# Second attention: the first sequence's output tiles projected inside the loop, and one PSUM bank for the output

## What is computed

```
q, k, v = x @ Wq, x @ Wk, x @ Wv        # 32 query heads, 8 key heads, head width 16
q, k = rope(q), rope(k)
scores = q @ k.T / 4, masked above the diagonal
ctx = softmax(scores) @ v               # (tokens, 512)
x = layernorm(x + ctx @ Wo)
# fourth block: x @ weight.T plus a low-rank part of two chosen experts out of eight
h = x @ gw1.T + gb1 ; gates from h ; x = layernorm(x + main + lora)
```

## Time and profile before

| what | value |
|---|---|
| median of 3 runs | 1127.17 us |
| profiled execution | 1127.07 us |
| its span, first to last instruction | 1125.3 us |
| TensorE busy | 1094.8 us (97%) |
| VectorE busy | 731.9 us (65%) |
| ScalarE busy | 635.4 us (56%) |
| GpSimd busy | 458.1 us (41%) |
| TensorE clock granted | 0.998 of full |
| loop of the third block | ends at 1045.34 us of the span |

### The profile page before, as it was taken

One profiled execution on the slowest core, in us unless ns is written; L12 is line 12 of the kernel. 1 busy time (PEld: TensorE's weight loads), 2 busy tenths in 40 slices (PEclk: granted clock), 3 DMA queues, 4 the chain that ended last, 5 costly groups with the idle time before them and its releaser, 6 DMA issues. The chain is left out here.

```text
span 1125.3 us, 19409 instructions
## 1 busy us (share of the span) xinstructions
PE 1094.8 (97%) x6288; PEld 898.7 (80%) x6288; DVE 731.9 (65%) x2384; ACT 635.4 (56%) x1487; POOL 458.1 (41%) x471
## 2 busy tenths in 40 slices
PE   7999999999999999999999999999999999999997
PEld 5888888888888888888888877888888875555786
DVE  6767776667776657776667776222242689997675
ACT  6656665556666556665566554454320237878424
POOL 4654554354544354553445251333310336345300
PEclk9999999999999999999999999999999999999999
DMA  6011110011111011110110000222200246661001
GB/s 240 20 38 39 38 39 29 13 38 38 39 38 29 13 47 38 32 35 29 28 30 20 29 1 24 80 75 69 96 5 1 36 55 86 92 110 20 1 1 75
DMA packets 28566, 49.72 MB, mean 44 GB/s; under 512 B 4400, under 2 KB 5552, under 8 KB 28464
## 3 DMA queue, kind: packets, MB, share of 16 engines
q1 hardware_dynamic: 27888, 47.41, 17.7%
q10 hardware_dynamic: 576, 1.05, 0.3%
HBM read 38.35 MB, written 2.10 MB: 36 GB/s over the span
## 5 line engine op out<-in xcount | busy, mean ns | idle before, releaser
L497 POOL TENSOR_TENSOR turned<-turned,sin 128x512 f32<-128x512 f32 x73 | 94.5, 1294 | 309.6 <-ACT turned L357 309.6
L373 ACT ACTIVATE probs<-probs,neg_max 128x256 f32<-128x256 f32 (+1 forms) x256 | 119.8, 473 | 11.3 <-DVE neg_max L590 11.3
L1748 DVE CUSTOM_DVE_ANT_0 a_unused<-bank,a_mask 128x512 bf16<-128x512 f32 (+3 forms) x256 | 109.1, 487 | 5.1 <-PE bank L1964 4.4
L500 POOL TENSOR_TENSOR turned<-turned,by_cos 128x512 f32<-128x512 f32 x73 | 101.2, 1386 | 5.7
L96 PE MATMUL bank<-wo_hi,oT_hi 128*128 128x512 f32 x256 | 100.3, 392 | 1.7 <-DVE oT_lo L653 1.7
L744 PE MATMUL bank<-xT_hi,wq_hi 128*128 128x512 f32 x256 | 101.5, 396 | 0.0
L744 PE MATMUL bank<-xT_lo,wq_hi 128*128 128x512 f32 x256 | 100.2, 391 | 0.0
L744 PE MATMUL bank<-xT_hi,wq_lo 128*128 128x512 f32 x256 | 100.1, 391 | 0.0
L96 PE MATMUL bank<-wo_hi,oT_lo 128*128 128x512 f32 x256 | 99.9, 390 | 0.0
L96 PE MATMUL bank<-wo_lo,oT_hi 128*128 128x512 f32 x256 | 99.7, 389 | 0.0
L432 ACT ACTIVATE pT_hi<-bank 128x512 fp32r<-128x512 f32 x112 | 61.7, 595 | 52.4 <-PE bank L783 52.4
(11 more groups left out here) (248 smaller groups left out, 3170.1 us busy)
## 6 DMA issues: line engine op xcount, KB each, us to landing
staged<-weights SPq DMA_DIRECT2D x70, 256.0 KB, 2.7
f_staged<-weights_f SPq DMA_DIRECT2D x33, 256.0 KB, 2.7
a_q_stack<-a_qT_hi SPq DMA_DIRECT2D x32, 128.0 KB, 3.4
rows<-x_rows SPq DMA_DIRECT2D x2, 1024.0 KB, 7.3
a_q_stack<-a_qT_lo SPq DMA_DIRECT2D x16, 128.0 KB, 3.9
out<-rows SPq DMA_DIRECT2D x8, 256.0 KB, 2.0
a_raw<-weights_qkv SPq DMA_DIRECT2D x4, 384.0 KB, 5.1
probs<-weights SPq DMA_DIRECT2D x4, 256.0 KB, 5.0
```

Of the source, the lines that this page charges most:

```text
L373: act.activation(probs[:, s % 2, h, 0:width], probs[:, s % 2, h, 0:width], ACT.Exp, bias=neg_max[:, s % 2, h:h + 1], scale=SCALE0, accum_o ...
L497: pool.tensor_tensor(at, at, sin[:, :], ALU.mult).then_inc(sin_done, 1)
L500: pool.tensor_tensor(at, at, by_cos_at(a, first), ALU.add).then_inc(roped, 1)
L1748: dve.tensor_tensor_reduce(unused[:, UNUSED_AT[qt]:UNUSED_AT[qt] + seen], ps_s[bank][:, at:at + seen], mask[:, SEQ - seen:SEQ], 1.0, LOWES ...
```

## The change

From slot 39 on, every 6 slots, one output tile of the first sequence is turned (`turn_early`, in the first of the 6 slots), split by ScalarE and VectorE in that slot, projected in four parts of 3 matmuls (`project_early`, in the third to sixth slot), and added to the rows by VectorE (`add_early`, in the sixth). All of this uses bank 7. So `ps_o` has bank 6 alone, `apply(u, 0)` waits for `join(u - 1)`, and `turn_tops` goes behind `apply` and writes into unused columns of bank 5, with a wait for that slot's exponentials; `key_scores` waits in its last piece of slots s % 4 = 2 for the copy of the tops. After the loop only tiles 4 to 7 are projected, the lists of three engines are reordered, and the fourth block's weight gets its high part from GpSimd instead of ScalarE. The diff, without the lines that only follow from `ps_o` being one bank, and with most removed lines of the last part left out (they stand in the kernel above):

```diff
@@ -1238,7 +1238,7 @@
...
-OUT_AHEAD = 58
+EARLY_FROM, EARLY_EVERY, EARLY_PARTS = 39, 6, 4
@@ -1367,9 +1367,10 @@
...
-        ps_s, ps_t, ps_o = psum[0:3], psum[3:6], psum[6:8]
-        ps_top = [psum[5]] + [ps_o[(u + 1) % 2] for u in range(1, UNITS1)]
+        ps_s, ps_t, ps_o = psum[0:3], psum[3:6], psum[6]
+        ps_top = [psum[5][:, 0:P]] + [psum[5][:, 2 * P:3 * P] for u in range(1, UNITS1)]
...
+        ps_early = psum[7]
@@ -1435,8 +1436,14 @@
...
+        def early_step(s):
+
+            tile, step = divmod(s - EARLY_FROM, EARLY_EVERY)
+            return (tile, step) if 0 <= tile < SEQ_TILES else (None, None)
...
+            bank = ps_early if tile < SEQ_TILES else ps_out[tile % 2]
@@ -1578,8 +1585,9 @@
...
-                if OUT_AHEAD <= s < OUT_AHEAD + SEQ_TILES:
-                    high_out(s - OUT_AHEAD)
+                tile, step = early_step(s)
+                if step == 0:
+                    high_out(tile)
@@ -1601,25 +1609,33 @@
...
-            act.wait_ge(main_raised, KC)
-            for k in range(KC):
-                act.activation(main_hi[:, k, :], main_raw[k], ACT.Copy).then_inc(main_hi_done, 1)
-            act.wait_ge(side_in, 32)
-            act.activation(b_hi[:, :], b_raw[:, :], ACT.Copy).then_inc(main_hi_done, 1)
-            for tile in range(TILES):
...
+            for tile in range(SEQ_TILES):
                 norm2.root(act, tile)
-                if tile >= 3:
-                    gate_root(tile - 3)
+            evacuate(UNITS1 - 1)
+            norm2.high(act, 0)
+            norm2.high(act, 1)
+            high_out(4)
+            high_out(5)
+            side_rows(0)
+            norm2.high(act, 2)
+            side_rows(1)
+            norm2.high(act, 3)
+            norm2.root(act, 4)
+            side_rows(2)
+            high_out(6)
+            norm2.root(act, 5)
+            side_rows(3)
+            high_out(7)
+            act.wait_ge(main_lo_done, KC)
+            norm2.high(act, 4)
@@ -1697,9 +1713,11 @@
...
             for k in range(KC):
+                pool.tensor_copy(main_hi[:, k, :], main_raw[k]).then_inc(main_hi_done, 1)
                 pool.wait_ge(main_hi_done, k + 1)
                 pool.tensor_tensor(main_lo[:, k, :], main_raw[k], main_hi[:, k, :].bitcast(F32),
                                    ALU.subtract).then_inc(main_lo_done, 1)
+            pool.tensor_copy(b_hi[:, :], b_raw[:, :]).then_inc(main_hi_done, 1)
@@ -1790,6 +1808,10 @@
...
+            def add_early(tile):
+                dve.wait_ge(y_ready, tile + 1)
+                dve.tensor_tensor(rows[:, tile, :], ps_early[:, :], rows[:, tile, :], ALU.add).then_inc(y_added, 1)
...
                 if s % GROUP1 == 1 and s >= 2 * GROUP1 + 1:
...
-                if OUT_AHEAD <= s < OUT_AHEAD + SEQ_TILES:
-                    low_out(s - OUT_AHEAD)
+                tile, step = early_step(s)
+                if step == 0:
+                    low_out(tile)
+                if step == EARLY_EVERY - 1:
+                    add_early(tile)
@@ -1813,12 +1838,15 @@
...
+            def take_stats(tile):
+                dve.wait_ge(y_added, tile + 1)
+                norm2.take(dve, tile)
+                norm2.moments(dve, tile)
@@ -1868,19 +1896,41 @@
...
-            for tile in range(TILES):
...
+            for tile in range(SEQ_TILES - 1):
+                take_stats(tile)
+            join(UNITS1 - 2)
+            take_stats(SEQ_TILES - 1)
+            for tile in range(SEQ_TILES):
                 norm2.scale(dve, tile)
-                if tile >= 3:
-                    gate_scale(tile - 3)
+            join(UNITS1 - 1)
+            norm2.split_low(dve, 0)
+            norm2.split_low(dve, 1)
+            low_out(4)
+            gate_rows(0)
+            low_out(5)
+            gate_rows(1)
+            norm2.split_low(dve, 2)
+            gate_scale(0)
+            gate_scale(1)
+            add_output(4)
+            norm2.split_low(dve, 3)
+            norm2.scale(dve, 4)
+            gate_rows(2)
+            low_out(6)
+            gate_scale(2)
+            add_output(5)
+            gate_rows(3)
+            norm2.scale(dve, 5)
+            low_out(7)
+            gate_scale(3)
+            add_output(6)
+            norm2.scale(dve, 6)
+            norm2.split_low(dve, 4)
+            add_output(7)
+            norm2.split_low(dve, 5)
+            gate_rows(4)
+            norm2.scale(dve, 7)
+            gate_scale(4)
@@ -1975,6 +2025,8 @@
...
+                if piece == PIECES - 1 and h == 2 and u + 1 < UNITS1:
+                    pe.wait_ge(top_ready, u + 2)
@@ -1987,14 +2039,9 @@
...
-                if u == 1:
-                    pe.wait_ge(v_done, TILES)
-                    pe.wait_ge(sin_done, 4 * TILES)
-                if u == 2:
-                    pe.wait_ge(part_lo, len(TURNS))
-                if u >= 3:
-                    pe.wait_ge(finished, u - 2)
-                pe.transpose(ps_top[u][:, 0:P], tops[:, u % 2, :], ident[:, :]).then_inc(top_turned, 1)
+                else:
+                    pe.wait_ge(exp_done, PIECES * (GROUP1 * u - 2))
+                pe.transpose(ps_top[u], tops[:, u % 2, :], ident[:, :]).then_inc(top_turned, 1)
@@ -2002,11 +2049,9 @@
...
-                if u == 1 and part == 0:
-                    pe.wait_ge(part_lo, len(TURNS))
                 if part == 0:
-                    if u >= 2:
-                        pe.wait_ge(finished, u - 1)
+                    if u >= 1:
+                        pe.wait_ge(finished, u)
@@ -2097,9 +2142,32 @@
...
+            def turn_early(tile):
+                pe.wait_ge(finished, KV1)
+                if tile >= 1:
+                    pe.wait_ge(y_added, tile)
+                for k in range(KC):
+                    mm = pe.transpose(ps_early[:, k * P:(k + 1) * P], o_tok[:, tile, k * P:(k + 1) * P],
+                                      ident[:, :])
+                mm.then_inc(out_turned, 1)
+
+            def project_early(tile, part):
+
+                at = slice(tile * P, (tile + 1) * P)
+                if part == 0:
+                    pe.wait_ge(w_lo_done, 3 * KC)
+                    pe.wait_ge(out_lo, tile + 1)
+                steps = [(a, b, k) for k in range(KC) for a, b in ((outT_hi, wo_hi), (outT_hi, wo_lo), (outT_lo, wo_hi))]
+                each = len(steps) // EARLY_PARTS
+                for n in range(part * each, (part + 1) * each):
+                    a, b, k = steps[n]
+                    mm = pe.matmul(ps_early[:, :], a[:, k, at], b[:, k, :], start=(n == 0), stop=(n == len(steps) - 1))
+                if part == EARLY_PARTS - 1:
+                    mm.then_inc(y_ready, 1)
@@ -2141,8 +2209,6 @@
...
-                if s % GROUP1 == 1 and s + 3 < SLOTS1:
-                    turn_tops((s + 3) // GROUP1)
@@ -2154,29 +2220,40 @@
...
+                if s % GROUP1 == 1 and s + 3 < SLOTS1:
+                    turn_tops((s + 3) // GROUP1)
...
-            pe.wait_ge(w_lo_done, 3 * KC)
-            for tile in range(TILES):
-                project_out(tile)
...
+                tile, step = early_step(s)
+                if step == 0:
+                    turn_early(tile)
+                if step is not None and step >= EARLY_EVERY - EARLY_PARTS:
+                    project_early(tile, step - (EARLY_EVERY - EARLY_PARTS))
+            turn_output(UNITS1 - 2)
+            for part in range(APPLY_PARTS):
+                apply(UNITS1 - 1, part)
+            norm2.turn(pe, 0)
+            norm2.turn(pe, 1)
+            turn_output(UNITS1 - 1)
+            pe.wait_ge(max_done, SEQ_TILES * SLOTS1)
+            turn_out(4)
+            pe.wait_ge(side_lo_done, KC)
+            side(0)
+            turn_out(5)
+            side(1)
+            norm2.turn(pe, 2)
+            project_out(4)
+            norm2.turn(pe, 3)
+            side(2)
+            turn_out(6)
+            project_out(5)
+            side(3)
+            turn_out(7)
+            project_out(6)
+            norm2.turn(pe, 4)
+            project_out(7)
+            norm2.turn(pe, 5)
+            side(4)
```

More of the change, by code:

```diff
@@ L1436, in maxima_before @@
             return ROW_TILES.index(qt) + 1
+        def early_step(s):
+            tile, step = divmod(s - EARLY_FROM, EARLY_EVERY)
+            return (tile, step) if 0 <= tile < SEQ_TILES else (None, None)
         def out_bank(tile):
-            return ps_out[tile % 2][:, :].rearrange("p (k c) -> p k c", k=KC)
+            bank = ps_early if tile < SEQ_TILES else ps_out[tile % 2]
+            return bank[:, :].rearrange("p (k c) -> p k c", k=KC)
         @block.sync
@@ L1602, in scale_last, with side_rows @@
                                scale=last.inv_deviation[:, tile:tile + 1]).then_inc(last.normed, 1)
[L1604 to L1622 removed]
+            def side_rows(tile):
+                low_rows(tile)
+                gate_root(tile)
+            for tile in range(SEQ_TILES):
+                norm2.root(act, tile)
+            evacuate(UNITS1 - 1)
```

(55 more changed lines are left out.)

21 lines of the change are left out of this document (6 added, 15 removed).

## The result

The changed kernel takes 1138.34 us (median of 4 runs, 1137.42 to 1140.88) against 1127.43 (1126.89 to 1127.84): a ratio of 1.0101, 95% interval 1.0082 to 1.0119. The profiled execution took 1137.5 us with a span of 1135.8; before it was 1127.07 with 1125.3. So 10.4 us came in between these two executions, where 10.2 were forecast; the forecast was 1137.

The account below looks back on a forecast made before the run. TensorE was taken as the bound, with VectorE nearly as full in the loop. Loop +14.2, last part -7.3, collision +2.0, entries +1.0 and tops +0.3 gave +10.2 on 1127.07: 1137 us, range 1130 to 1143.

Parts of the forecast that it names:

- The bound: Slots 39 to 63: TensorE's 3.0 us of stand-still is all that moved work can fill; the loop grows by 14.2 us.
- 1.0 for entries: TensorE entering another kind of matmul, for 16 parts of the moved projection: 1.0 us, bounds 0 to 3.2.
- hand-made schedule: Slots 39 to 63, each engine in its order, timed from slot 39's start: 5.9 us of stand-still, end at 63.1.
- The last part: From the loop's end to the gates' transposition: 11.1 us of matmuls leave, 4.0 of stand-still comes, -7.3 us.
- the collision: Behind the loop, GpSimd's casts and subtractions delay VectorE's four norm2.scale before join(15): 2.0 us, bounds 0 to 4.7.
- no collision, 1135 us: Rival: behind the loop GpSimd's casts fall between VectorE's scales, all else as forecast; 1135 us (1131 to 1138), chance 0.20.
- The tops: The moved turn_tops and its copy in the loop: 0.3 us, bounds 0 to 6.
- Slots 9 to 38 I leave as they are: Loop before early projecting: no change, since turn_tops waited for the same join at the place where apply waits now.
- a sign of being wrong: Stated beforehand: the prediction would be wrong if slots 9 to 38 take another time than before the change.
- rival of late tops (+6): Tops' transfer 0.75 us late in eight units of slots 9 to 39, the loop slips: 1143 us, chance 0.13.
- Faster: Rival: loop loses nothing and the last part has no holes either: -3.0 us, 1124 us, chance 0.04.
- gaps filled: Rival: VectorE hides its copies, loop work 57.2 against 48.87; with a last part that waits 1128 us, chance 0.08.

Follow-up runs that it names:

- e1_low_later: The changed kernel with VectorE's low_out of an early tile one slot later, behind the next slot's maxima; 1.28 us less between turn_output of units 7 and 14.

## Why the forecast held, and where it was off

- **The bound.** The loop grew by 15.0, with 14.2 and some of the 1.0 for entries forecast, and the new waits stand in the slots that were named. The hand-made schedule can be held against the trace from slot 39's start: `apply(9, 0)` 6.15 (said 6.3), the first tile's last projecting matmul ends at 15.34 (15.3), the loop's end 63.9 (63.1 before entries). Head-of-line waits in VectorE's list, an instruction that waits and holds up those behind it, are shown by three kernels, with 2.0 us that a mere reordering takes back.
- **The last part.** -5.65 against -7.3 + 2.0. The waits were 0.81 for `evacuate(14)` (said 0.85), 0.81 for `join(14)` (1.4: VectorE's statistics were just done, so the part of it for its order fell away), 0.85 for `join(15)` (1.0, and the collision's 2.0 ahead of it), 0.53 before `side(4)` (0.6). That is 3.0 us of stand-still where 6.0 were said; another 1.6 went into `apply` of unit 15 at half the clock, a term that the sum didn't have. In e1_low_later, without the half clock, the waits come to 4.1 and the last part takes 31.10, -5.9. The work beside the waits takes 1.0 to 1.3 more than the 25.7 that the forecast left it (36.98 - 11.1 - 0.2); the sum had 1.0 for entries, in a term of its own. That the forecast of the last part agrees to 0.3 is in part luck: too much stand-still stood against a half clock and longer work.
- **The collision.** The size was right: 1.9 on four instructions, said 2.0. Its worth on the path was not: GpSimd held back gave 1.34 at the first `side`, and at the gates 0.10, because its last three instructions then met `gate_scale`. The rival "no collision, 1135 us" is therefore not excluded as a mechanism, since seven of GpSimd's ten instructions ran beside VectorE without loss there; but by these figures a list that avoids both places would win some 1.3 us, not 2.0 (an estimate; not run).
- **The tops.** The mis-sized step: 0.3, measured 0.7 in A (0.5 to 1.3 over nine traces of the same code). "Slots 9 to 38 I leave as they are" was wrong, and the prediction had named another time there as a sign of being wrong. So was its reason: I compared the `join` that both kernels wait for, and not the place of `turn_tops` behind `apply` and behind the slot's exponentials, which the diff adds as a wait. Their own bank, ahead of `apply`, takes 2.2 us out of A. The rival of late tops (+6) named a late transfer; only two in slots 8 to 36 came too late for the keys, 0.5 us of wait. The loss was TensorE's own stand at `turn_tops` and at `apply`.
- **The clock.** It was not in the sum. In both profiled executions of the changed kernel its stretch lay where the collision held VectorE anyway, 0.24 us; seven of the ten executions took 1.5 to 3.5 us longer, at a lower mean clock. The forecast of 1137 is therefore that of an execution of the first kind (1137.4 to 1137.6), and the median of 1138.3 holds some of the others.
- **Faster or gaps filled** did not come: by the prediction's own count of the loop's work (57.2) TensorE's stand-still there grew from 3.0 to 6.7 us, and even with every wait that these runs found reordered the kernel stays at 1131.6.

## What to carry to other kernels

When work moves into a loop whose engines are both nearly full, count the room of the loop (3.0 us here) against what moves (11.1), and then look at what stands at the head of each list: a copy that waits for another engine holds the join behind it, and a single buffer passes that on at once. Two uses that share a bank set each other's order: a bank of their own for the tops, and with it a place ahead of `apply`, was worth 2.2 us in slots 8 to 36, and with that the output's second bank was missed only where a `join` stood late in VectorE's list. Moving a helper's work away from one collision is worth nothing if it lands on the next: look up which of the other engine's instructions it will run beside. Covering a wait can be worth more than the wait, since a sparse stretch of TensorE may be followed by 3.4 us at half the granted clock (1.98 us of waiting cost 3.6).

## What the runs showed of the hardware

- TensorE's granted clock fell to 0.50 (1.2 GHz) behind stretches with some work in them (busy 0.43, 0.66 and 0.29 of three microseconds; 0.17 of 2.00 us and then 1.3 us of work in another kernel; 0.94 and 0.80 of two microseconds in a third), and came back to 1.00 after some 3.4 us; `apply` of unit 15 took 3.94 us in it and 2.36 without. The Trainium skill, "TensorE: Matmul & The Clock Gate", "Part 1: The HAM clock gate", has recent activity decide between these two levels. These rows show the two levels; that the same waits came with and without the fall, no run here explains.
- VectorE's small instructions collide with GpSimd too: 128x32 took 1.07 instead of 0.30 us beside a subtraction of 128x512 on GpSimd. In each collision here VectorE's instruction ended shortly behind GpSimd's, 0.28 us at 128x512 and about 0.04 at 128x32, so that the price went by what was left of GpSimd's instruction. VectorE's copies out of a PSUM bank kept their 0.69 us beside the same subtractions.
